# Adjacency product with residual and normalisation: other piece sizes in the last loop turn and the small groups, and the last row's variance from a centred product

## What is computed

```python
keep = (u >= 0.1).astype(x.dtype)
x_drop = x * keep / 0.9
y = x + adj @ x_drop
out = (y - mean(y)) / sqrt(var(y) + 1e-5)     # over the 64 columns of each row
```

## Time and profile before

| | |
|---|---|
| median of 3 runs | 641.6 us (641.6 to 641.93) |
| the profiled execution | 641.38 us |
| its span, first to last instruction | 639.8 us |
| TensorE matmul / VectorE / ScalarE busy | 80% / 9% / 3% |
| moved by DMA | 274.8 MB, mean 430 GB/s |
| chain that ended last | DMA 66%, TensorE 33% |

### The profile page before, as it was taken

How to read it: one execution, slowest core, us unless ns; L and a number is a source line. 1 busy time by engine, 2 the same in 40 slices (tenths; PEclk the granted TensorE clock), 3 DMA queues, 4 the chain that set the end, 5 groups by cost and what they waited for, 6 DMA issues and landing times.

```text
span 639.8 us, 7684 instructions
## 1 busy us (share of the span) xinstructions
PE 510.9 (80%) x3458; PEld 263.8 (41%) x3458; DVE 60.8 (9%) x268; ACT 17.0 (3%) x24; POOL 1.1 (0%) x8
## 2 busy tenths in 40 slices
PE   0098798798788888887978778978978977979897
PEld 0044444444444443443434434434533533445435
DVE  1200100100100100100010100010020020020202
ACT  0000000000000000000000000000000000000000
POOL 0000000000000000000000000000000000000000
PEclk9997978978988988987979978978978977989999
DMA  9999999999999999999999999999999999999998
GB/s 385 430 431 447 427 430 451 430 430 443 434 434 397 438 449 416 438 430 443 430 430 451 430 430 443 438 430 399 451 446 407 435 430 446 428 432 419 430 421 368
DMA packets 7348, 274.80 MB, mean 430 GB/s; under 512 B 944, under 2 KB 1072, under 8 KB 1456
## 3 DMA queue, kind: packets, MB, share of 16 engines
q1 hardware_dynamic: 7200, 274.70, 99.6%
q10 hardware_dynamic: 144, 0.03, 0.0%
HBM read 272.63 MB, written 2.10 MB: 429 GB/s over the span
## 4 chain that ended last, share of the span: by engine, by line
DMA 66%; PE 33%; issue 0%; SPq 0%; DVE 0%; ACT 0%; ACTq 0%; DVEq 0%
DMA adj_ring<-adj_blocks 66%; PE acc L228 31%; PE tail_acc L228 2%; PE back L235 0%; SPq L148 0%; PE final L267 0%; SPq L150 0%; DVE x_and_u L335 0%; SPq L169 0%; ACT std L219 0%; DVE acc_sb L273 0%; ACTq L197 0%; DVE stats L329 0%; DVE mean_var L331 0%; DVE rstd L333 0%
## 5 line engine op out<-in xcount | busy, mean ns | idle before, releaser
L228 PE MATMUL acc<-adj_ring,x_and_u 128*64 128x320 f32 x3072 | 463.9, 467 | 98.2 <-ACTq L197 98.1
L228 PEld LDWEIGHTS acc<-adj_ring,x_and_u 128*64 128x64 f32 x3072 | 232.2, 148 | 324.9 <-ACTq L197 106.6
L273 DVE COPY acc_sb<-acc 128x320 f32<-128x320 f32 x24 | 10.7, 486 | 474.6 <-PE acc L228 474.6
L228 PE MATMUL tail_acc<-adj_ring,x_and_u 128*64 128x384 f32 (+1 forms) x256 | 29.1, 382 | 2.0 <-DMA adj_ring<-adj_blocks 1.9
L235 PE MATMUL back<-twofold,acc_sb 128*128 128x64 f32 x126 | 16.8, 280 | 11.9 <-DVE acc_sb L273 11.9
L191 ACT ACT_TABLE_LOAD x10 | 12.8, 1283 | 502.4 <-DMA adj_ring<-adj_blocks 502.4
L235 PEld LDWEIGHTS back<-twofold,acc_sb 128*128 128x128 f32 x126 | 15.0, 191 | 18.8 <-DVE acc_sb L273 18.6
L228 PEld LDWEIGHTS tail_acc<-adj_ring,x_and_u 128*64 128x64 f32 x256 | 15.7, 137 | 15.2 <-issue 9.8
L304 DVE TENSOR_SCALAR x_and_u<-summed,mean,rstd 128x64 f32 (+1 forms) x63 | 15.2, 309 | 0.5
L242 PE MATMUL final<-x_and_u,identity 128*128 128x64 f32 x2 | 0.7, 432 | 13.2 <-DMA x_and_u<-xu 13.2
L282 DVE BATCH_NORM_STATS2 stats<-summed 128x6 f32<-128x64 f32 x63 | 9.3, 213 | 0.4
(11 more groups left out here) (17 smaller groups left out, 7.4 us busy)
## 6 DMA issues: line engine op xcount, KB each, us to landing
adj_ring<-adj_blocks SPq DMA_DIRECT2D x23, 7680.0 KB, 33.3
adj_ring<-adj_blocks SPq DMA_DIRECT2D x11, 5120.0 KB, 36.8
adj_ring<-adj_blocks SPq DMA_DIRECT2D x1, 5760.0 KB, 27.8
adj_ring<-adj_blocks SPq DMA_DIRECT2D x1, 4480.0 KB, 29.8
x_and_u<-xu SPq DMA_DIRECT2D x1, 4096.0 KB, 12.3
adj_ring<-adj_blocks SPq DMA_DIRECT2D x1, 3840.0 KB, 24.8
adj_ring<-adj_blocks SPq DMA_DIRECT2D x1, 3072.0 KB, 31.7
adj_ring<-adj_blocks SPq DMA_DIRECT2D x1, 2560.0 KB, 35.5
```

The lines of the kernel that those rows point to most:

```text
L228: return nc.tensor.matmul(into[h * D:(h + 1) * D, 0:cols], x_drop[:, t * D:(t + 1) * D], adj_ring[:, at:at + cols], start=(t < 2), stop=(t ...
L273: last = nc.vector.tensor_copy(acc_sb[:, b * cols:(b + 1) * cols], part[:, 0:cols])
```

## The change

The piece sizes of the last loop turn become 20, 20, 14, 10. The small groups are loaded in four pieces each: 24, 18, 12, 10 tiles for three rows and 20, 20, 14, 10 for the last one. The sizes of the pieces in `WAITS` follow, so that TensorE waits at six k tiles in each turn (0, 20, 24, 40, 48, 54) where it waited at five (0, 24, 42, 48, 56).

The last row is centred in the products. GpSimd makes `centred`, `twofold` less 1/64 in every element, so that a product with it subtracts the mean over the 64 columns. VectorE takes the mean of the last row of x at the start, behind the dropout work, and subtracts it into `last_x`, which the first product puts into `final` in place of the row of x. So `final` holds the row less its mean. ScalarE squares it, with the sum of the squares as a second output, and takes the root of sum / 64 + eps. VectorE's statistics and aggregation at the end are gone, and the last scaling multiplies by the reciprocal alone.

```diff
@@ -21,7 +21,7 @@
 SLOTS = len(SLOT_TILES)
 
 
-LAST_TILES = [24, 18, 14, 8]
+LAST_TILES = [20, 20, 14, 10]
 LAST_FIRST = [sum(LAST_TILES[:i]) for i in range(len(LAST_TILES))]
 WAITS = sorted(set(SLOT_FIRST + LAST_FIRST))
 MAIN = FULL * SLOTS
@@ -31,7 +31,7 @@
 COLS = TILE // 2
 SPLIT = TILE // COLS
 
-TAIL = [(3, [20, 16, 12, 10, 6]), (1, [16, 18, 14, 10, 6])]
+TAIL = [(3, [24, 18, 12, 10]), (1, [20, 20, 14, 10])]
 LAST = len(TAIL) - 1
 FIRST_ROW = [FULL * R + sum(rows for rows, _ in TAIL[:n]) for n in range(len(TAIL))]
 FIRST_PIECE = [sum(len(tiles) for _, tiles in TAIL[:n]) for n in range(len(TAIL))]
@@ -92,6 +92,10 @@
         normed = x_nat
         identity = sb("identity", [P, P])
         twofold = sb("twofold", [P, D])
+        centred = sb("centred", [P, D])
+        last_x = sb("last_x", [P, D])
+        last_squares = sb("last_squares", [P, 1])
+        deviations = sb("deviations", [P, D])
         eps = sb("eps", [P, 1])
         acc_sb = sb("acc_sb", [P, TILE])
         summed = sb("summed", [P, R * D])
@@ -141,6 +145,8 @@
         final_stats = sem("final_stats")
         final_var = sem("final_var")
         out_stored = sem("out_stored")
+        centred_ready = sem("centred_ready")
+        x_centred = sem("x_centred")
 
         def sync_program(sp):
             def load(s, group):
@@ -184,6 +190,9 @@
 
             pool.wait_ge(identity_ready, 1)
             nc.gpsimd.tensor_tensor(twofold[:], identity[:, 0:D], identity[:, D:P], ALU.add).then_inc(twofold_ready, 1)
+
+            pool.wait_ge(twofold_ready, 1)
+            nc.gpsimd.tensor_scalar(centred[:], twofold[:], 1.0 / D, None, ALU.subtract).then_inc(centred_ready, 1)
 
         def scalar_program(act):
             def root(n, rows):
@@ -215,8 +224,11 @@
             root(FULL - 1, R)
             for n in range(LAST):
                 root(FULL + n, TAIL[n][0])
+
+            act.wait_ge(final_ready, 1)
+            nc.scalar.activation(deviations[:], final[:, 0:D], ACT.Square, accum_out=last_squares[:]).then_inc(final_var, 1)
             act.wait_ge(final_var, 1)
-            nc.scalar.activation(std[:, 0:1], mean_var[:, 1:2], ACT.Sqrt, bias=eps[:]).then_inc(std_ready, 1)
+            nc.scalar.activation(std[:, 0:1], last_squares[:, 0:1], ACT.Sqrt, scale=1.0 / D, bias=eps[:]).then_inc(std_ready, 1)
             act.wait_ge(normed_ready, FULL + LAST + 1)
             cols = slice((KT - 1) * D, KT * D)
             act.dma_start(out_rows[:, cols], normed[:, cols]).then_inc(out_stored, 16)
@@ -238,8 +250,9 @@
 
             pe.wait_ge(twofold_ready, 1)
 
-            pe.wait_ge(x_loaded, 16)
-            nc.tensor.matmul(final[:, 0:D], identity[:], x_nat[:, (KT - 1) * D:KT * D], start=True, stop=False)
+            pe.wait_ge(x_centred, 1)
+            nc.tensor.matmul(final[:, 0:D], identity[:], last_x[:], start=True, stop=False)
+            pe.wait_ge(centred_ready, 1)
             with pe.Fori(0, FULL) as g:
                 for s in range(SLOTS):
                     for pair in range(SLOT_FIRST[s], SLOT_FIRST[s] + SLOT_TILES[s], 2):
@@ -264,7 +277,7 @@
 
                         turn_back(TAIL[n - 1][0], FULL + n - 1)
             pe.wait_ge(acc_copied, FULL + LAST + 1)
-            nc.tensor.matmul(final[:, 0:D], acc_sb[:, 0:P], twofold[:], start=False, stop=True).then_inc(final_ready, 1)
+            nc.tensor.matmul(final[:, 0:D], acc_sb[:, 0:P], centred[:], start=False, stop=True).then_inc(final_ready, 1)
 
         def vector_program(dve):
             def take(into, cols, used):
@@ -316,6 +329,13 @@
                 dve.wait_ge(kept_ready, i + 1)
                 nc.vector.tensor_scalar(x_drop[:, cols], x_drop[:, cols], 1.0 / (1.0 - P_DROP), None,
                                         ALU.mult).then_inc(drop_ready, 1)
+
+            cols = slice((KT - 1) * D, KT * D)
+            nc.vector.bn_stats(stats[:, 0, :], x_nat[:, cols]).then_inc(final_stats, 1)
+            dve.wait_ge(final_stats, 1)
+            nc.vector.bn_aggr(mean_var[:], stats[:, 0, :]).then_inc(final_stats, 1)
+            dve.wait_ge(final_stats, 2)
+            nc.vector.tensor_scalar(last_x[:], x_nat[:, cols], mean_var[:, 0:1], None, ALU.subtract).then_inc(x_centred, 1)
             with dve.Fori(0, FULL) as g:
                 take(acc, COLS, (g + 1) * SLOTS)
                 normalise(g, g * R, R)
@@ -325,15 +345,11 @@
                 normalise(FULL + n, FIRST_ROW[n], rows)
 
             take([tail_acc[LAST]], P, MAIN + FIRST_PIECE[LAST] + len(TAIL[LAST][1]))
-            dve.wait_ge(final_ready, 1)
-            nc.vector.bn_stats(stats[:, 0, :], final[:, 0:D]).then_inc(final_stats, 1)
-            dve.wait_ge(final_stats, 1)
-            nc.vector.bn_aggr(mean_var[:], stats[:, 0, :]).then_inc(final_var, 1)
             dve.wait_ge(std_ready, FULL + LAST + 1)
             nc.vector.reciprocal(rstd[:, 0:1], std[:, 0:1]).then_inc(rstd_ready, 1)
             dve.wait_ge(rstd_ready, FULL + LAST + 1)
-            nc.vector.tensor_scalar(normed[:, (KT - 1) * D:KT * D], final[:, 0:D], mean_var[:, 0:1], rstd[:, 0:1],
-                                    ALU.subtract, ALU.mult).then_inc(normed_ready, 1)
+            nc.vector.tensor_scalar(normed[:, (KT - 1) * D:KT * D], final[:, 0:D], rstd[:, 0:1], None,
+                                    ALU.mult).then_inc(normed_ready, 1)
 
         sync_program(nc.sync)
         gpsimd_program(nc.gpsimd)
```

## The result

| | before | changed |
|---|---|---|
| median of 12 runs | 641.62 us | 642.95 us |
| lowest and highest | 641.44 to 641.93 | 641.59 to 644.25 |
| profiled execution, its span | 641.38, 639.8 | 644.23, 642.3 |

The ratio is 1.0021, 95% interval 1.0013 to 1.0029: slower by 1.3 us in these runs. Two of the twelve runs are as fast as before (641.6), the profiled one is among the slowest.

What follows compares the result with a forecast made beforehand. The prediction took the DMA stream of the matrix as the bound, with TensorE already limiting the last row by 0.3 us. Terms +0.9 - 0.05 + 0 = +0.85 us gave 642.2, put at 642.4 us, range 641.5 to 643.6.

Steps and rivals of the forecast that it cites:

- The small groups: Three-row group and last row: a larger last three-row piece makes TensorE start the last row late, +0.9 us.
- the start of a piece: TensorE in the small groups: starting a piece that was waited for costs 0.1 us more than its tiles' pace.
- One piece fewer: Stream ahead of the last three-row landing: one piece fewer, bounded by 0 and -0.1 us, taken as -0.05.
- The stream still sets the end: Rival, last row: TensorE catches up and the last landing sets the end, +0.15, 641.7 us; chance 0.12.
- The last turn: Last loop turn: TensorE waits 4.3 us, the turn ends at 601.2 to 603.3, cost 0.
- The chain: Steps behind TensorE's last product: Square with its sum replaces statistics, 0.49 against 0.48 us, cost 0, bounds -0.15 and +0.25.
- the rival of the second store's landing: End of span: second store lands at 639.45, so a shorter chain alone cannot go below 641.0; no chance of its own.
- The table load: Rival, chain on ScalarE: Square and perhaps the root load tables, 1.28 us each, 643.7 or 645.0; chance 0.06.
- The low clock: Rival, between the last turn's end and 606.4: clock falls to 1.2 GHz, end 0.4 to 1.1 us later; chance 0.13.
- a fall in the last turn closes this gap: Argument against the low clock: a fall in the last turn makes it end late, closing the gap before the small groups.

Runs made afterwards that it cites:

- e11: The changed kernel run once more without an edit, in a later group of runs; median 642.35 us, ratio 1.0003 to the kernel before.
- e2: Kernel before with only the small groups' pieces changed, to 24, 18, 12, 10 and 20, 20, 14, 10; median 642.41 us, ratio 1.0014.
- e6: Kernel before with only the last row's pieces changed, to 20, 20, 14, 10; median 641.69 us, ratio 1.0002.
- e10: Kernel before with only the three-row group's pieces changed, to 24, 18, 12, 10; median 642.43 us, ratio 1.0004.
- e1: Kernel before with only the last loop turn's pieces changed, to 20, 20, 14, 10; median 641.55 us, ratio 1.0000.
- e3: Changed kernel with all piece sizes as before, so only the centred last row is left; median 641.64 us, ratio 1.0003.
- e7: Kernel before with the first store of the result cut to 64 of its 3840 columns; median 641.44 us.
- e8: Changed kernel with all piece sizes as before and the first store cut to 64 columns, centred row kept; median 641.38 us.
- e5: Changed kernel with the last loop turn's pieces back at 24, 18, 14, 8; median 642.52 us.
- e12: Changed kernel with the last loop turn's pieces back at 24, 18, 14, 8, run a second time; median 642.36 us, ratio 1.0007.
- e4: Changed kernel with TensorE kept busy by products into an unused PSUM tile around the turn back; median 641.68 us, ratio 1.0004.

## Why the prediction was right in size and wrong in its reasons

The forecast was 642.4 us in 641.5 to 643.6, and the median is 642.95. That is within the range, and the kernel is slower by 1.3 us where +0.85 was forecast. In the second group, e11, it was 642.35, slower by 0.84. The steps did not fare so well.

- **The small groups, +0.9 us: the term was three times too large.** e2 measures +0.3 (636.17 against 635.90), e6 (636.25) and e10 (636.27) +0.35 and +0.37, each with one group changed. The order of events was right: the wait for the last three-row piece (624.65), no wait worth naming after it, the turn back at 630.21. The sizes were off. The piece landed at 624.65 and not 624.85, from there to the turn back it was 5.56 us and not 5.73, the turn back took 0.81 and not 0.88, and the last 44 tiles 5.02 and not 5.2. Behind two of these stands one misreading, of the timeline's "unbroken row" in the kernel before. The weight loads of the same stretch show that TensorE waited in it for landings (start us, us, idle before):

```profile
622.01 0.20 PEld L228 LDWEIGHTS tail_acc<-adj_ring,x_and_u 128*64 128x64 f32 x4 [1.17 <-DMA adj_ring<-adj_blocks]
622.38 0.14 PEld L228 LDWEIGHTS tail_acc<-adj_ring,x_and_u 128*64 128x64 f32 x2 [0.18 <-issue]
...
627.28 1.73 PEld L228 LDWEIGHTS tail_acc<-adj_ring,x_and_u 128*64 128x64 f32 x32 [0.56 <-DMA adj_ring<-adj_blocks]
...
632.25 3.29 PEld L228 LDWEIGHTS tail_acc<-adj_ring,x_and_u 128*64 128x64 f32 x60 [0.24 <-DMA adj_ring<-adj_blocks]
```

  Between tiles of three rows the loads idle for 0.18 us; the 0.56 at 627.28 is a wait of some 0.38 us for the last row's first piece. So the 0.1 us that I took for the start of a piece was this wait, less what the start saved: a piece that is waited for starts two tiles in 0.37 us. And 0.119 us a tile held waits too, as at 632.25: e10, with the same pieces of the last row but a start 0.62 us later, took 5.46 us for the same 48 tiles, 0.114 each.
- **One piece fewer, -0.05: not shown.** The last three-row piece landed 0.1 to 0.2 us sooner than forecast (624.65 in e2, 624.75 in e10), but a piece that no edit touched was started at 622.00 to 622.26 in five profiles (before, e1, e3, e7, e8).
- **The stream still sets the end, given 0.12.** Not in the changed kernel: its last 84 and 44 tiles run without a wait. But the argument against this rival, 0.119 us without a break, was the misread row: before, landings still held TensorE in the last row, by 5.72 less 5.46 = 0.26 us.
- **The last turn, 0: right.** TensorE waited 4.16 us in its middle (I had 4.3) and ended it at 603.3 (601.2 to 603.3). The runs of e1, e5 and e12 show no cost.
- **The chain, 0: it saved 0.2 us that do not arrive.** Square and the handing over of the sum take 639.53 to 639.88 = 0.35 us against 0.48, the last scaling with its issue 0.32 against 0.37 (1.39 less 1.19 is 0.20 in all). Square took 0.22 us, where I set a floor of 0.30 from the roots. The Trainium skill (ScalarE: Activation LUTs, What ACT_TABLE_LOAD costs) has 186 ns + 0.833 ns an element for immediate scale and bias, by which 64 elements are an estimated 239 ns, next to the 0.22 us measured; no run here varies the bias. Of the 0.20 us nothing arrives. In e3 the stores that drain take it, as the rival of the second store's landing said; I had that as a floor at 641.0, and no run of e3 went below 641.52. In the changed kernel, whose end comes later, the last store lands in 1.5 us, so the span should keep the gain, but there as in e3 some 0.2 us come in outside the span. That was no term of the sum.
- **The table load** did not come: between ScalarE's Square and root there is nothing but the reading of the sum, and the changed kernel's profile has ten loads as before, the last at 517 us.
- **The low clock, given 0.13: this is what happened**, in 18 of 23 runs of the changed kernel if "above 642.0" is the mark. All seven profiles with this three-row group bear the mark out: the four above 642.0 have a low clock between 606 and 612, the three below have none. The place was right, between the end of the last turn and 606.4. The condition failed. I took the longest single wait that had kept the clock, 2.08 us, as the measure, but the second wait was 1.18, 1.19, 1.95 and 2.60 us in the four executions that fell and 1.43, 1.48 and 1.65 in the three that did not (the last with the products of e4 ahead of it). A single wait is no measure: the stretch had a first wait of 0.99 us and only the small products of the turn back in it. The price was half of the story. I assumed some 3 us at the lower level and an end 0.4 to 1.1 us later; e11 and e5 had that, 0.5 and 0.9 later. But in the changed kernel's first profile it was 6 us, 606.79 to 612.8, so 3.0 us lost, and the top of the runs is 644.25 and not 643.5. The argument "a fall in the last turn closes this gap" held for the gap's length (1.19 us) and not for the outcome.

The sum came out well since the first error, 0.6 us too much, stood in for nearly half of the clock's cost, 642.95 less the 641.6 of the runs that are as fast as before. That is luck and no merit of the sum.

What stays open: what decides the fall and its length, as equal kernels go either way; whether the last turn shifts the share of falls a little, which 23 runs of each cannot tell; and where the 0.2 us outside the span come from.

## What to carry to other kernels

Where TensorE is only a little faster than the stream that feeds it, plan the pieces by the gaps that they leave and not only by what is left after the last byte: larger pieces in one group opened a gap of 1 to 2.6 us and put 3 to 6 us at the half clock on the path, in most runs, and fewer issues returned nothing that shows. A row of products that the timeline prints as one can still hold waits; the weight loads of the same stretch show them. When a change widens the spread of the runs while the lowest stay, look for a state that is drawn anew in each execution before pricing instructions. And before shortening the last steps, look at what else must land: 0.2 us saved ahead of a store were worth nothing while 2 MB of other stores drained. Compare the spans and the times of the runs as well: where the span shrank by 0.2 us, the time did not.

## What was not expected of the hardware

- The granted clock fell to 0.50 around waits of 0.99 and 1.19 us with a turn back of 1.33 us between them, and stayed at 1.00 in e2 around 0.99, 1.33 and 1.43 us. With the same waits it was low for some 6 us in one execution of the changed kernel and for some 3 us in another (e11).
- Products into an unused PSUM tile (1.0 us before, 1.3 us behind the turn back) kept it at 1.00 in the profiled execution, and 10 of 11 runs stayed under 642.0. The median was 641.68 us against 641.51 before.
- ScalarE's sum of a Square is a second instruction of 0.19 us that starts 0.12 us after the first; the root follows 0.35 us after the Square began.
- The last store, 32 KB, took 1.8, 1.6 and 1.5 us to land when issued at 637.90, 638.10 and 638.37, behind 2 MB of other stores.
